# A semaphore of its own for the sums, row maxima issued one bank at a time, and the last group's scores in pairs

## The reference

```python
qkv = jnp.einsum('btc,oc->bto', x, w_attn)
q, k = _apply_rope(q, cos, sin), _apply_rope(k, cos, sin)
scores = jnp.einsum('bhqd,bhkd->bhqk', q, k) / jnp.sqrt(hd)
attn = jax.nn.softmax(jnp.where(causal, scores, -jnp.inf), axis=-1)
y = jnp.einsum('bhqk,bhkd->bhqd', attn, v)
y = y + gating[0] * softmax(q @ ak / sqrt(C)) @ av            # adapter, 10 keys
x = _layernorm(x + jnp.einsum('btc,oc->bto', y, w_proj))
base_out = jnp.einsum('bsi,oi->bso', x, base_w) + base_b
combine = top 2 of softmax(x @ router_w.T), normalised
delta = jnp.einsum('bse,bsr,eor->bso', combine, x @ A.T, B)
x = _layernorm(x + base_out + delta * 0.5)
```

## Time and profile before

| | us |
|---|---|
| median of 3 runs | 905.51 (902.58 to 906.15) |
| profiled execution, its own time | 910.93 |
| its span, first to last instruction | 909.2 |
| TensorE matmuls busy | 863.0 (95%) |
| VectorE busy | 694.2 (76%) |
| ScalarE busy | 442.9 (49%) |
| GpSimd busy | 294.2 (32%) |
| mean granted TensorE clock | 0.945 |

### The profile page before, as it was taken

How to read it: one execution, slowest core, us unless ns; L and a number is a source line. 1 busy time by engine, 2 the same in 40 slices (tenths; PEclk the granted TensorE clock), 3 DMA queues, 4 the chain that set the end, 5 groups by cost and what they waited for, 6 DMA issues and landing times.

```text
span 909.2 us, 15822 instructions
## 1 busy us (share of the span) xinstructions
PE 863.0 (95%) x5240; PEld 547.3 (60%) x5240; DVE 694.2 (76%) x2149; ACT 442.9 (49%) x836; POOL 294.2 (32%) x375
## 2 busy tenths in 40 slices
PE   9999989999999999998999999999986999999997
PEld 6788858765454444444444444443455888888875
DVE  5865677798889879797797988997256776767767
ACT  4233323235467868687686886887541111110110
POOL 0222211222023525253253443554222543333321
PEclk9999999999689979799797998998998999999999
DMA  7324361645134442245423444321311011010110
GB/s 262 116 83 150 96 200 59 203 117 121 30 69 95 87 92 63 56 92 129 90 60 64 90 96 84 76 84 36 126 37 37 24 46 46 23 46 25 45 35 35
DMA packets 44945, 75.53 MB, mean 83 GB/s; under 512 B 15244, under 2 KB 16716, under 8 KB 44876
## 3 DMA queue, kind: packets, MB, share of 16 engines
q1 hardware_dynamic: 44876, 74.66, 32.1%
HBM read 48.31 MB, written 21.23 MB: 76 GB/s over the span
## 4 chain that ended last, share of the span: by engine, by line
PE 71%; DVE 12%; SPq 5%; issue 4%; ACT 3%; DMA 2%; POOL 1%; DVEq 0%
PE bank L1769 14%; PE bank L1638 11%; PE bank L531 11%; PE bank L533 10%; PE bank L532 10%; PE bank L1653 9%; DVE mx L1218 3%; DVE bank L1215 3%; PE bank L1586 2%; SPq L572 2%; SPq L678 2%; SPq L684 1%; ACT pt L1068 1%; PE bank L1602 1%; DVE xtl L1332 1%
## 5 line engine op out<-in xcount | busy, mean ns | idle before, releaser
L1068 ACT ACTIVATE pt<-bank 128x512 f32<-128x512 f32 x576 | 304.3, 605 | 117.5 <-PE bank L1638 112.9
L1215 DVE CUSTOM_DVE_ANT_0 bank<-bank,cmask 128x128 f32<-128x128 f32 (+2 forms) x464 | 204.3, 500 | 30.3 <-PE bank L1653 28.0
L1638 PE MATMUL bank<-qs,ks 50*128 50x512 f32 (+3 forms) x768 | 208.4, 396 | 3.0 <-ACT pt L1068 2.5
L1769 PE MATMUL bank<-pt,vb 128*32 128x512 f32 (+3 forms) x1536 | 176.5, 551 | 6.5 <-POOL pt L843 3.3
L1653 PE MATMUL bank<-ks,qs 48*128 48x512 f32 (+3 forms) x720 | 168.0, 417 | 10.4 <-DVE mx L1218 6.4
L1638 PEld LDWEIGHTS bank<-qs,ks 50*128 50x128 f32 x768 | 111.6, 196 | 95.8 <-ACT pt L1068 76.1
L843 POOL TENSOR_SCALAR_AFFINE_SELECT pt<-pt 128x512 f32<-128x512 f32 (+1 forms) x160 | 84.6, 548 | 215.4 <-ACT pt L1068 214.1
L1653 PEld LDWEIGHTS bank<-ks,qs 48*128 48x128 f32 x720 | 88.8, 198 | 95.4 <-DVE mx L1215 28.9
L1218 DVE TENSOR_REDUCE mx<-bank 128x1 f32<-128x512 f32 x208 | 130.5, 682 | 15.0 <-PE bank L1653 14.4
L763 POOL TENSOR_TENSOR part<-rope,part 128x1024 fp32r<-128x1024 f32 x16 | 38.2, 2390 | 164.5 <-ACT part L929 164.5
L1021 ACT CAST xth<-bank 128x512 fp32r<-128x512 f32 x15 | 8.8, 587 | 140.6 <-PE bank L1829 140.6
(11 more groups left out here) (197 smaller groups left out, 1481.6 us busy)
## 6 DMA issues: line engine op xcount, KB each, us to landing
qs<-q_parts SPq DMA_DIRECT2D x34, 256.0 KB, 4.0
ks<-k_parts SPq DMA_DIRECT2D x34, 256.0 KB, 6.8
q_parts<-part SPq DMA_DIRECT2D x32, 256.0 KB, 3.3
k_parts<-part SPq DMA_DIRECT2D x32, 256.0 KB, 3.4
qs<-q_parts SPq DMA_DIRECT2D x34, 128.0 KB, 4.9
ks<-k_parts SPq DMA_DIRECT2D x34, 128.0 KB, 5.7
yv<-yts SPq DMA_DIRECT2D x128, 32.0 KB, 2.1
rspread<-dens SPq DMA_DIRECT2D x64, 64.0 KB, 2.2
```

What stands on the lines that cost most here:

```text
L1068: act.activation(pt[k % PT_BUFS][:, h], half(n % SCORE_BUFS), ACT.Exp, scale=float(HD) ** -0.5).then_inc(S("exp_done"), 1)
L1215: last = ve.tensor_tensor_reduce(blk, blk, cmask[:, BANK - nk * P:], 1.0, NEG, ALU.add, ALU.max, mx[m][:, 0, h, qt:qt + 1])
L1638: last = pe.matmul(half(n % SCORE_BUFS)[:, col:col + n_], ks[slot_of(g)][r0:r0 + KX, h // 2, kb * P:(kb + 1) * P], qs[slot_of(g)][r0:r0 + ...
L1769: last = pe.matmul(values_out[VW * h:VW * h + VW, BANK - n_:], vb[g % 2][:, kb, h, :], pt[(NS * g + st) % PT_BUFS][:, n, col:col + n_], st ...
```

## The change

The sums' four transfers get a semaphore of their own, den{i}_moved. `invert` waits for it alone; `evac_y` waits for both, and `divide` now waits for y{i}_moved itself. Maxima are issued one bank at a time by MAX_AT (35 banks of a table; the order of banks differs by half and head pair, and the first is of the odd half), VALUES_AT, COPY_AT and INVERT_AT are redrawn, the copies of EXCESS banks follow their place, and group 0 starts its maxima at up to 4/3 a chunk. On GpSimd a group goes by chunks: the negation at chunk 22, the splits of the projection's weights at 28, both divisions after all else of the group. In the last group TensorE issues scores two chunks at a time in four banks (3, 0, 1, 2), then what is due of V-steps and of the first tiles; its tables are redrawn too, and the splits of y stand at chunks 20 and 28, behind the masks of 19 and 27. `invert(14)` moves ahead of `lo_x(0, 0)` and `norms(1, 1)`.

```diff
-BANK_ORDER = [[0, 1, 2, 3, EXCESS, 4, 5, 6, JOINED], [EXCESS, 0, 1, 2, 3, 4, 5, 6, JOINED]]
+BANK_ORDER = [[[2, 1, 0, 3, EXCESS, 5, JOINED, 4, 6], [2, 0, 6, 1, 5, 4, EXCESS, 3, JOINED]],
+              [[2, 4, EXCESS, 3, 6, 0, 5, JOINED, 1], [3, 4, 6, 0, 5, EXCESS, 2, 1, JOINED]]]
...
-EXCESS_AT = [2, 7, 20, 23]
-NEGATE_STEP = 5
+NEGATE_AT = 22
...
     pr, r = divmod(w, 2 * NMB)
-    return pr, r % 2, MAX_BANKS[BANK_ORDER[pr][r // 2]]
+    return pr, 1 - r % 2, MAX_BANKS[BANK_ORDER[pr][r % 2][r // 2]]
...
-VALUES_AT = [10, 12, 16, 19, 26, 30, 31, 33, 38, 41]
-COPY_AT = [17, 42]
-PAIRS_AT = [0, 2, 3, 3, 6, 8, 10, 11, 15, 16, 17, 21, 22, 25, 29, 31, 33, 34]
-INVERT_AT = 20
-DIVIDE_STEPS = [6, 8]
+VALUES_AT = [8, 12, 17, 22, 25, 27, 32, 35, 38, 41]
+COPY_AT = [18, 42]
+MAX_AT = [0, 0, 2, 3, 4, 5, 5, 6, 8, 8, 8, 9, 10, 11, 12, 13, 15, 16, 17, 17, 19, 20, 20, 22, 22, 23, 25, 26, 29, 30, 30, 32, 33, 34, 35, 35]
+INVERT_AT = 21
...
-LAST_VALUES_AT = [8, 10, 13, 17, 20, 22, 25, 28, 32, 36]
-LAST_COPY_AT = [14, 42]
+LAST_VALUES_AT = [9, 11, 17, 21, 23, 25, 29, 31, 35, 36]
+LAST_COPY_AT = [18, 42]
+LAST_BANKS = [3, 0, 1, 2]
...
-PROJ_AT = [(4, 9, 14, 15), (19, 21, 24, 26)]
-X_AT, ROUTER_AT = 26, (30, 33)
+PROJ_AT = [(1, 7, 7, 13), (15, 19, 27, 27)]
+X_AT, ROUTER_AT = 25, (31, 33)
...
-    return min(FIRST[c], max(0, 2 * ((c - LEAD_CHUNKS[-1] - 2) // 2)))
+    return min(FIRST[c], max(0, 4 * (c - LEAD_CHUNKS[-1] - 2) // 3))
...
+        def score_out(g, c):
+            return half(LAST_BANKS[c % len(LAST_BANKS)] if g == G - 1 else (g * SCORE_BANKS + c) % SCORE_BUFS)
...
                     sp.dma_start(den[VW * h + a0:VW * h + a0 + VW // 2], ...
-                                 ).then_inc(S(f"y{i}_moved"), 16)
+                                 ).then_inc(S(f"den{i}_moved"), 16)
...
                 gp.wait_ge(S("den_spread"), 16 * HG * (g + 1))
+                gp.wait_ge(S(f"y{i}_moved"), 16 * HG * (g + 1))
...
+                if g >= 2 and g % 2 == 0:
+                    divide(g // 2 - 1, 0)
+                    divide(g // 2 - 1, 1)
...
                 if g > 0:
-                    act.wait_ge(S(f"y{i}_moved"), 16 * 2 * HG * g)
+                    act.wait_ge(S(f"den{i}_moved"), 16 * HG * g)
+                    act.wait_ge(S(f"y{i}_moved"), 16 * HG * g)
...
                 for i in range(2):
-                    ve.wait_ge(S(f"y{i}_moved"), 16 * 2 * HG * (g + 1))
+                    ve.wait_ge(S(f"den{i}_moved"), 16 * HG * (g + 1))
...
+            invert(G - 2)
             lo_x(0, 0)
             norms(1, 1)
-            invert(G - 2)
...
+                if g == G - 1 and c == 0:
+                    pe.wait_ge(S("max_read"), reads_before(MAX_TOTAL))
+                elif g == G - 1:
+                    pe.wait_ge(S("exp_done"), n + 1 - len(LAST_BANKS))
...
+            def pe_last():
+                for c in range(0, SCORE_BANKS, 2):
+                    score(G - 1, c)
+                    score(G - 1, c + 1)
+                    for n in (c, c + 1):
+                        if n + SCORE_BANKS in VALUES_AT:
+                            weighted(G - 2, VALUES_AT.index(n + SCORE_BANKS))
+                        if n in LAST_VALUES_AT:
+                            weighted(G - 1, LAST_VALUES_AT.index(n))
+                        first_tiles(n)
```

More of the change, by code:

```diff
@@ L198, in place_slots @@
         first.append(slot)
-        for _ in range(PAIRS_AT.count(c)):
+        for _ in range(MAX_AT.count(c)):
             if tiles == NMX - LEAD:
@@ L204, in place_slots @@
                 slot += 1
-            slot, tiles = slot + 2, tiles + 2
+            slot, tiles = slot + 1, tiles + 1
     assert slot == SLOTS and tiles == NMX
@@ L282 @@
 KEEP_CHUNKS = [2, 4, 6, 8]
-KEEP_PAIRS = [17, 22]
+KEEP_MAXIMA = [17, 22]
 LEAD_FIRST = 3
 LEAD_CHUNKS = [2]
-PROJ_AT = [(4, 9, 14, 15), (19, 21, 24, 26)]
-X_AT, ROUTER_AT = 26, (30, 33)
+PROJ_AT = [(1, 7, 7, 13), (15, 19, 27, 27)]
+X_AT, ROUTER_AT = 25, (31, 33)
 HIGH_X_AT, ROUTER_EXP_AT = 26, 35
-SPLIT_Y_STEPS = [4, 7]
+SPLIT_Y_AT = [20, 28]
 SPLIT_GROUPS = [7, 9, 11, 13]
-SPLIT_STEP = 7
+SPLIT_AT = 28
 PROJ_BANK, X_BANK, ROUTER_BANK, FF_BANK = 4, 5, 2, (7, 6)
@@ L812, in negate_q @@
                 gp.wait_ge(S("excess_copied"), excess_before(g))
-                gp.wait_ge(S("diag_masked"), len(MASKED) * (g - 1) + sum(tile_of(i) < NEGATE_STEP for i in MASKED))
+                gp.wait_ge(S("diag_masked"), len(MASKED) * (g - 1) + sum(last_chunk(i) <= NEGATE_AT for i in MASKED))
                 for par in range(2):
@@ L850, in gp_group @@
                     split_y(1, 1)
-                for st in range(NS):
-                    if g in SPLIT_GROUPS and st == SPLIT_STEP:
+                for c in range(SCORE_BANKS):
+                    if g in SPLIT_GROUPS and c == SPLIT_AT:
                         split_proj(SPLIT_GROUPS.index(g))
-                    for i in range(len(slots_with(excess, g))):
-                        if EXCESS_AT[i] // HG == st:
+                    for i, slot in enumerate(slots_with(excess, g)):
+                        if EXCESS_CHUNK[slot] == c:
                             mask_excess(g, i)
-                    if st == NEGATE_STEP and g + 1 < G and slots_with(excess, g + 1):
-                        negate_q(g + 1)
[L859 to L867, removed]
+                    if g == G - 1 and c in SPLIT_Y_AT:
+                        split_y(2 + SPLIT_Y_AT.index(c), SPLIT_Y_AT.index(c))
+                    for i in MASKED:
+                        if last_chunk(i) == c:
+                            mask_diagonal(g, i)
+                            if i == LAST_VALUE[0] and g + 1 < G:
+                                build_v(g + 1)
+                    if c == NEGATE_AT and g + 1 < G and slots_with(excess, g + 1):
+                        negate_q(g + 1)
+                if g >= 2 and g % 2 == 0:
+                    divide(g // 2 - 1, 0)
+                    divide(g // 2 - 1, 1)
             for g in range(G):
@@ L1067, in act_group @@
                     act.wait_ge(S("score_full"), n + 1)
-                    act.activation(pt[k % PT_BUFS][:, h], half(n % SCORE_BUFS), ACT.Exp,
+                    act.activation(pt[k % PT_BUFS][:, h], score_out(g, c), ACT.Exp,
                                    scale=float(HD) ** -0.5).then_inc(S("exp_done"), 1)
@@ L1637, in score @@
                     r0, n_ = HALF * (h % 2), width(hf, kb)
-                    last = pe.matmul(half(n % SCORE_BUFS)[:, col:col + n_], ks[slot_of(g)][r0:r0 + KX, h // 2, kb * P:(kb + 1) * P],
+                    last = pe.matmul(score_out(g, c)[:, col:col + n_], ks[slot_of(g)][r0:r0 + KX, h // 2, kb * P:(kb + 1) * P],
                                      qs[slot_of(g)][r0:r0 + KX, h // 2, (hf + 1) * BANK - n_:(hf + 1) * BANK], start=True, stop=True)
@@ L1781, in pe_group @@
                     for slot in range(slots[c], slots[c + 1]):
-                        if not held(g, slot) or g == G - 1:
+                        if not held(g, slot):
                             continue
@@ L1787, in pe_group @@
                             n, w = max_tile(slot)
-                            if g == 0 and c in KEEP_PAIRS and slot == slots[c]:
+                            if g == 0 and c in KEEP_MAXIMA and slot == slots[c]:
                                 keep_on(free_bank(use_of(g, slot)), 2 * P)
                             group_max(g + n, w, use_of(g, slot))
-                    if g == G - 1:
-                        first_tiles(c)
                     if g == 0 and c in KEEP_CHUNKS:
@@ L1858, in first_tiles @@
                     if c in PROJ_AT[t]:
-                        proj(t, t, [PROJ_AT[t].index(c)])
-            for g in range(G):
+                        proj(t, t, [n for n in range(CC) if PROJ_AT[t][n] == c])
+            for g in range(G - 1):
                 pe_group(g)
+            pe_last()
             for i in range(NPV):
```

6 lines of the change are left out of this document (2 added, 4 removed).

## The result

The median is 873.94 us (869.1 to 875.04, four runs) against 905.83 us (902.58 to 913.18, four runs) on the same chip: a ratio of 0.963, 95% interval 0.956 to 0.970. The profiled execution took 874.05 us, its span 872.3 us, 36.9 us less than the 909.2 of before; the medians differ by 31.9 us.

The account below looks back on a forecast made before the run. It blamed VectorE's stalls before reciprocals with their half-clock stretches, and the last group's chains. Terms -24 - 4 - 11 = -39 us on 910.93 gave 871.9; that execution being 5.4 above the median, 867 us, range 849 to 891.

Parts of the forecast that it names:

- The semaphore and INVERT_AT, -24: Groups behind the first: VectorE's stalls before reciprocals and the half-clock stretches go, -24 us, bounds -28 and -10.
- at least one reduction of some 0.65 us later than 313.6: Group 3: the reciprocal, a slot later and behind chunk 20, comes past the sums' landing at 314.0, so no stall.
- The third rival: Sums queue behind the load as values do, so half the stalls stay, with their clock: 890 us, chance 0.12.
- The half-clock stretch goes with the stall: Attention groups: removing VectorE's stall before the reciprocal also removes the clock's fall, 3.1 us an ordinary pair of groups.
- the five longer ones did: Of six stalls before reciprocals, the five longer brought a half-clock stretch; the one of 0.48 us did not.
- Tables, -4: Attention groups: redrawn tables and maxima issued singly pair matmuls on opposite halves, -0.3 us a group, -4 us together.
- -1.55 as the bound: Quiet groups: VectorE's busy time, 47.73 in 50.82 us, is the floor, so at most -1.55 us a group.
- pairs of matmuls (0.34 against 0.42 us): TensorE: two matmuls on different halves take 0.34 us to the next start, a lone score 0.42 us.
- Divisions at the end: Divisions behind every mask of a group still end before SyncE's next load: cost nothing, at worst 1 us of 20.
- Last group and reciprocals, -11: Kernel's end: shorter last group and earlier reciprocal 14 bring reciprocal 15 to 671 from 682.43, -11 us, bounds -5 and -15.
- Near 32 us: Last group, first score to last V-step: paired scores, less TensorE idle and less half clock, 39.1 - 7.2 = 32 us.
- the likeliest case: The forecast itself, the three gains together giving 867 us, chance 0.49.

Follow-up runs that it names:

- x5: The kernel before with only the sums' own semaphore added: 901.36 us, 0.982 of before.
- x1: The changed kernel with the sums counted on the values' semaphore again: 884.63 us, 0.960 of before.
- x7: The changed kernel with INVERT_AT 23 instead of 21, the reciprocal two reductions later: 861.88 us, 0.942 of before.
- x3: The changed kernel with the last group's single scores, three banks and tables as before, reciprocal 14 still early: 873.90 us, 0.951 of before.
- x6: The changed kernel with the loads of the first two x tiles issued ahead of those of B: 865.05 us, 0.948 of before.
- y1: The changed kernel itself, unaltered, measured again on another chip: 871.08 us, 0.962 of before.
- y2: The changed kernel with INVERT_AT 23 and the first x loads ahead of those of B: 854.50 us, 0.944 of before.
- y3: y2 with group 7's first weights' load issued behind the sums and y of group 6: 844.99 us, 0.933 of before.
- y4: The changed kernel with V-steps and copies (VALUES_AT, COPY_AT) at the old slots: 916.42 us, 1.010 of before.
- x8: The changed kernel with the previous group's sums and values issued ahead of the q and k load, groups 1 to 14: 943.10 us, 1.033 of before.
- x2: The changed kernel with maxima in pairs, bank order and INVERT_AT as before, new V-steps kept: 925.76 us, 1.011 of before.

## Why the prediction was right in sum and wrong in its terms

I forecast 867 us, -39 on the profiled execution of before; the profiled spans differ by -36.9. By medians it is -31.9, and 873.94 is 7 us above the 867. The terms:

- **The semaphore and INVERT_AT, -24: about -13 in the groups, and not by this way.** The step that failed is "at least one reduction of some 0.65 us later than 313.6". I measured the reciprocal's place in reductions from its old time, with the load held still. In the new order VectorE comes to it 0.7 us earlier, counted from the load, and eight places stall for 10.7 us in all. x5 and x1 price the semaphore at 4 and 6 us. x7 shows that the place was the matter: two reductions later, most of the stalls are gone. The third rival named this (sums behind the load, the reciprocal earlier), but with it the falls of the clock were to stay, and three of five went.
- **"The half-clock stretch goes with the stall": too strong.** In before the clock goes to 0.50 at 318.22, 372.83, 427.44, 488.88 and 543.50 us, 3.0 to 4.6 us after the start of a stall of 1.39, 1.73, 4.79, 0.83 and 1.63 us, and stays there for 10.24 us, at 427.44 for 17.07. Those were my five. After has eight stalls in the thirteen groups, two followed by a fall (that of 4.18 us, and of 1.36 us at 466.43). Ten traces have old V-steps with old maxima or new with new, and the load in its place: before, after, x1, x3, x5, x6, x7, y1, y2, y3. They have 23 falls in their thirteen groups, and each begins within 11 us of the start of a stall of 0.6 us or more before a reciprocal. All eleven stalls of 2 us or longer have such a fall, twelve of the forty between 0.5 and 2 us, and no shorter one; y3, without the long stall, has none at all. So a long stall was followed by a fall each time and a short one mostly not, where I had read "the five longer ones did" as always. Only y3 tests this by taking the stall away. Nor is a stall needed: y4 and x8 have none before a reciprocal, and seven and eleven falls.
- **What else stands ahead of a fall.** Mostly it is a short idle time of TensorE, whatever it waited for: 0.41 us before 318.22, 0.77 before 491.29. In the ten traces 18 of the 23 falls have such a gap of 0.41 to 3.12 us in the 5 us ahead of them. But it is not enough. Of ten such gaps of 0.77 or 0.78 us that y4 has between 316 and 600 us, five had a fall soon behind them (320.62, 402.54, 436.67, 491.29, 549.31 us) and five had none. In after, TensorE's gaps before the transposes of the row maxima are 0.46 to 0.85 us in eight groups, without a fall; those of 2.33 and 1.20 us stand right ahead of the two falls:

```profile
315.88 0.27 PE L1682 MATMUL bank<-ident,mneg 128*64 128x128 f32 x1 [0.85 <-DVE mneg L1240]
...
417.88 0.27 PE L1682 MATMUL bank<-ident,mneg 128*64 128x128 f32 x1 [2.33 <-DVE mneg L1240]
...
471.36 0.27 PE L1682 MATMUL bank<-ident,mneg 128*64 128x128 f32 x1 [1.20 <-DVE mneg L1240]
```

  Nor is such a gap needed: the three falls of x5 have none over 0.35 us in those 5 us. No run shows what the clock goes by, and why one gap and not its twin stays open. The clock gave about 15 of the 36.9 us, 13 of them in the thirteen groups, where I had 15 (and 9 for the stalls).
- **Tables, -4: some -15.** In the thirteen groups 27.9 less 13 for the clock leaves 15 us, 1.1 us a group, with the stalls unchanged. I took -0.3 and kept -1.55 as the bound; quiet pairs went from 50.82 us to between 48.44 and 48.72, -1.1 to -1.2 a group. For its size this is the term that I mis-sized most. The bound was not even one: VectorE's busy time in such a pair is now 45.6 to 46.9 us, not 47.73, by overlap and not by less work, so the busy time of one order is no floor for another. With x7 the pairs take 47.9. Four kernels show that both tables are needed: with the sums on their own semaphore, old V-steps and old maxima give 867 at equal clock, or 864 with the new last group, worth 3 (x5); new V-steps with old maxima 878 (x2); old V-steps with new maxima 875 (y4); both new 852. Each half of the table alone loses 11 to 14 us, both together gain 12. x5 also keeps the divisions and reciprocal 14 at their old places, which no run priced, so these three figures are rough. I had asked of pairs of matmuls (0.34 against 0.42 us). By VectorE's waits for banks, 31.9 us before, 77.7 in x2, 71.6 in y4 and 13.5 after, what counts is whether TensorE comes to fill the bank that VectorE waits for; which place of a V-step does it was not tried.
- **Divisions at the end, "cost nothing, at worst 1 us": about so.** The forecast followed them to the next load_group, which group 14 has not, and not to what SyncE issues there instead. In after they hold SyncE for 1.2 us there. But the 4.96 us of TensorE are not theirs: x1, x2, x7, x8 and y1 have the divisions in the same place, SyncE is not held, and TensorE stands 4.44, 4.20, 4.59, 4.07 and 3.12 us. In x7:

```profile
588.22 2.45 SPq L682 DMA_DIRECT2D den<-yts  x4
590.72 2.48 SPq L688 DMA_DIRECT2D yv<-yts  x4
```

```profile
605.46 0.76 PE L535 MATMUL bank<-wph,qs 128*128 128x512 f32 x1 [4.59 <-issue]
```

- **Last group and reciprocals, -11: about -7, 1.5 of it clock.** "Near 32 us" from first score to last V-step fell: 38.85, with the new wait of 4.96 and 2.37 for the last exponential. The step that failed is that the redrawn tables were priced without asking when x lands. Tile 1's projection now begins two chunks behind the end of tile 0's (15 behind 13, before 19 behind 15), and x, still issued behind B, lands 14.8 us after the group's first score, 11.4 before. With the old tables (x3) the wait is not there, and with x issued ahead of B it is gone and the group takes 31.3 us (x6). What the last group gained without that is its start, 5.1 us behind the last row maxima and not 8.8. From the last row maxima to the last copy it is 44.0 us (48.1 before), from there to the first delta 14.1 (17.4). Reciprocal 15 is no longer held by the values (2.35 us of wait for the sums, 7.56 before), and TensorE's gap before the first delta is 2.80 us, as forecast. Reciprocal 14 came at 620.22 and not 666.68. x3 gives pairs and tables 3 us; the rest is the start and the reciprocals, by subtraction.

So the likeliest case did not happen as told: two terms were too large by some 11 and 4 us, one too small by 11, and 1.7 us ahead of group 2 were not forecast. That the sum came out near is luck: the errors cancelled. A sum that comes out does not vouch for its terms.

## What to carry to other kernels

Two tables that share an engine's slots are one edit: price them together, or change them together and measure; each half of this one alone loses. Time the place of a waiting instruction from the transfer that it waits for, not from its own old time, since a faster order moves the two apart. Before moving a transfer or an operation that others wait for in a queue worked in order, list for each group what is issued behind it, the last group and the one before it above all. Before asking for a result sooner, look when its last input lands.

## What was not expected of the hardware

The span follows the time at half clock by 0.35 us per us, and executions of one kernel differ widely in it: before had 85 to 153 us at half clock in 33 executions, y3 10 to 27 in four. GpSimd's division of 1.29 us (598.09) took 3.12 us at 601.99 and the addition of 1.29 us (605.18) took 2.37 at 599.45, while VectorE split weights (L1318 and L1320, 599.45 to 603.96). The first load of x landed 9.1 us after its issue behind the two transfers of B, and 2.8 us after it ahead of them (x6). And a gap of 0.77 us of TensorE, the same in ten groups of y4, was followed by a half-clock stretch in half of them only.
